# A graph layer in float32 on one core: paired row statistics, ScalarE roots, a SiLU stage of its own, and the mean taken off on VectorE

## The reference, cut to what matters

```python
def _layernorm(x, axis=-1, eps=1e-05):
    m = jnp.mean(x, axis=axis, keepdims=True)
    v = jnp.var(x, axis=axis, keepdims=True)
    return (x - m) / jnp.sqrt(v + eps)

h = jnp.maximum(_layernorm(x), 0.0)          # relu of the normalised rows
x = x + layer0(h, node_vec1, edge_attr_4, edge_attr_8, ...)
h = jnp.maximum(_layernorm(x), 0.0)
x = x + layer1(h, edge_attr_4, ...)          # h + relu(sum of messages)

# in layer0, per edge, the small net that weights the messages:
hid = jax.nn.silu(edge_scalars @ fc_w1 * (1.0 / np.sqrt(8.0)))     # 8 -> 64
weight = hid @ fc_w2 * (1.0 / np.sqrt(64.0))                       # 64 -> 192
# and per node
angle = 0.1 * (mid_s @ lin3_w) * (1.0 / np.sqrt(96.0)) * node_attr
out = jnp.cos(angle) * scfeat + jnp.sin(angle) * conv
```

## Time and profile before

| | |
|---|---|
| median of 3 runs | 2483.28 us (2479.98 to 2484.08) |
| span of the profiled execution | 2863.6 us |
| busy, of the span | PE 1940.9, PEld 1820.7, DVE 1954.7, ACT 1560.1, POOL 1745.2 us |
| instructions | PE 12874, DVE 8628, ACT 4412, POOL 1676 |
| moved | 364.52 MB |

### The profile page before, as it was taken

How to read it: one execution, slowest core, us unless ns; L and a number is a source line. 1 busy time by engine, 2 the same in 40 slices (tenths; PEclk the granted TensorE clock), 3 DMA queues, 4 the chain that set the end, 5 groups by cost and what they waited for, 6 DMA issues and landing times.

```text
span 2863.6 us, 55863 instructions
## 1 busy us (share of the span) xinstructions
PE 1940.9 (68%) x12874; PEld 1820.7 (64%) x12874; DVE 1954.7 (68%) x8628; ACT 1560.1 (54%) x4412; POOL 1745.2 (61%) x1676
## 2 busy tenths in 40 slices
PE   0888888878878888878883343434344777777877
PEld 0777777777877777777773333323233777767777
DVE  2889888887888888888884655556555444444444
ACT  0667677776777777777774444545453222222222
POOL 1656666665666666766656565655565666666665
PEclk9989999998999999999995555555555999999898
DMA  9444544443444444454543232323332333333332
GB/s 79 142 143 169 172 170 171 172 172 138 169 172 170 173 169 164 162 179 147 180 154 124 87 89 87 93 87 97 88 99 83 81 89 88 92 92 90 94 95 74
DMA packets 223602, 364.52 MB, mean 127 GB/s; under 512 B 115938, under 2 KB 133149, under 8 KB 223405
## 3 DMA queue, kind: packets, MB, share of 16 engines
q1 hardware_dynamic: 176524, 289.81, 32.1%
q0 software_dynamic: 47040, 74.31, 9.8%
HBM read 176.85 MB, written 194.78 MB: 130 GB/s over the span
## 4 chain that ended last, share of the span: by engine, by line
DVE 31%; PE 25%; issue 14%; another core or an unknown queue 11%; POOL 8%; ACT 6%; SPq 2%; DMA 1%; DVEq 1%; ACTq 0%; POOLq 0%
DVE st L1334 3%; PE bank L969 3%; PE bank L1154 3%; POOL x_e L581 3%; POOL inv L628 3%; DVE x L1353 2%; DVE su_e L1203 2%; PE bank L964 2%; PE bank L1166 2%; DVE st L1362 2%; PE bank L1163 2%; ACT h L755 2%; PE bank L1176 2%; DVE x L1599 2%
## 5 line engine op out<-in xcount | busy, mean ns | idle before, releaser
L628 POOL TENSOR_TENSOR inv<-var,minus_half 128x8 f32<-128x8 f32 x196 | 327.7, 1672 | 256.5 <-DVE var L1210 253.4
L625 POOL TENSOR_TENSOR yo<-x,h 128x640 f32<-128x640 f32 x196 | 305.8, 1560 | 147.8 <-ACT h L755 145.4
L969 PE MATMUL bank<-wp,hT 128*128 128x160 f32 x1568 | 392.6, 334 | 1.6 <-DVE x L1353 0.7
L755 ACT ACTIVATE h<-x,nmr,inv 128x160 f32<-128x160 f32 x784 | 342.2, 514 | 6.1 <-POOL nmr L642 6.1
L587 POOL DMA_INDIRECT h_all<-h,i_put x196 | 203.4, 1038 | 217.9 <-ACT h L871 146.0
L964 PE MATMUL bank<-ident,h_e 128*128 128x128 f32 x392 | 83.0, 350 | 358.9 <-ACT h_e L878 229.2
L587 POOL DMA_INDIRECT out<-yo,i_put x196 | 202.1, 1031 | 197.2 <-DVE feat L1706 63.8
L1353 DVE SCALAR_TENSOR_TENSOR x<-bank,scl,x_all 128x160 f32<-128x160 f32 x784 | 254.3, 372 | 89.1 <-PE bank L970 46.0
L969 PE MATMUL bank<-wp,eT 128*128 128x160 f32 x784 | 274.5, 444 | 54.5 <-ACT eR L886 27.3
L934 ACT ACTIVATE tot<-bank 128x160 f32<-128x160 f32 x196 | 59.6, 304 | 455.7 <-remote 207.1
L964 PEld LDWEIGHTS bank<-ident,h_e 128*128 128x128 f32 x392 | 57.5, 184 | 367.9 <-DVE hr_e L1215 244.1
(11 more groups left out here) (173 smaller groups left out, 6292.4 us busy)
## 6 DMA issues: line engine op xcount, KB each, us to landing
x_all<-in_xa SPq DMA_DIRECT2D x98, 644.0 KB, 5.8
h_all<-h SPq DMA_DIRECT2D x98, 640.0 KB, 2.9
out<-yo SPq DMA_DIRECT2D x98, 640.0 KB, 3.3
q_row<-row_tab SPq DMA_DIRECT2D x98, 256.0 KB
sum_tab<-tot SPq DMA_DIRECT2D x49, 322.0 KB, 4.2
y_tab<-yo SPq DMA_DIRECT2D x49, 320.0 KB
x<-y_tab SPq DMA_DIRECT2D x49, 320.0 KB
cv<-sum_tab SPq DMA_DIRECT2D x25, 322.0 KB
```

The lines of the kernel that those rows point to most:

```text
L625: nc.gpsimd.tensor_tensor(yo[j][:, a:b], x1[j][:, a:b], h1[j][:, a:b], ALU.add).then_inc(d_y, 1)
L628: nc.gpsimd.tensor_tensor(inv[:, 0:n], var[:, 0:n], minus_half[:, 0:n], ALU.pow).then_inc(signal, 1)
L755: ins = nc.scalar.activation(h1[j][:, k * D:(k + 1) * D], x1[j][:, k * D:(k + 1) * D], ACT.Relu, bias=nmr2[j][:, k:k + 1], scale=inv2[j][: ...
L969: nc.tensor.matmul(dst_ps, main[:, t * P:(t + 1) * P], wp[:, w:w + D], start=True, stop=False)
```

## The change

The statistics take two rows at once: the access pattern interleaves them (element 0 of row g, element 0 of row g+1, element 1 of row g, ...), so that the even half of `bn_stats` is the one row and the odd half the other. No combining is left. The root is `Sqrt` on ACT with scale 1/160 and bias eps, the inverse a `reciprocal` on DVE (in stage 1 for the dense rows; the edge rows keep the power on POOL). For dense rows and in stage 2, DVE subtracts the mean from all 160 columns; for the edge rows of stage 1 POOL does. The relu moves into the copy behind the transpose. The net's inner product and SiLU for all 49 quads stand in a stage of their own ahead of stage 1, in 13 groups, and go to a table in HBM (`hid_tab`) from which each quad loads its 128 x 256 part, behind its table loads.

```diff
-            def moment_part(part, st, su, df, sq, m2, neg, var, n, signal):
...
-            def rest_of(into, rows, neg, n, signal):
...
+            def paired_stats(st, pair, rows, width):
+                two_rows = rows[:, 2 * pair * width:(2 * pair + 2) * width].rearrange("p (g f) -> p f g", f=width)
+                return V.bn_stats(st[:, 2 * pair:2 * pair + 2, :].rearrange("p g k -> p (g k)"), two_rows[:, 0:D, :])
+            def shift_of(nmr, st, inv, n, signal):
+                V.scalar_tensor_tensor(nmr[:, 0:n], stat(st, n, 1), -1.0, inv[:, 0:n], ALU.mult, ALU.mult).then_inc(signal, 1)
...
             def dense_stats(u):
-                for k in range(GD):
-                    ins = V.bn_stats(st1[j][:, k, :], x_in[j][:, k * XW:k * XW + D])
+                for pair in range(GD // 2):
+                    ins = paired_stats(st1[j], pair, x_in[j], XW)
...
+            def dense_centre(u):
+                j, x = u.mod(2), x3(x_in[u.mod(4)], XW, GD)
+                v.wait_ge(d_ln1, u.times(1, 1))
+                wait(v, d_tr, u.times(2, -2))
+                V.tensor_tensor(x3(hb[j], P, GD), x[:, :, 32:D], bc_last(stat(st1[u.mod(4)], GD, 1), P), ALU.subtract)
+                V.tensor_tensor(x3(hr[j], 32, GD), x[:, :, 0:32], bc_last(stat(st1[u.mod(4)], GD, 1), 32),
+                                ALU.subtract).then_inc(d_cen, 1)
+            def dense_inverse(u):
+                v.wait_ge(d_sq1, u.times(1, 1))
+                V.reciprocal(inv1[j][:, :], sd1[j][:, :]).then_inc(d_scl, 1)
+            def dense_scale(u):
+                v.wait_ge(d_scl, u.times(2, 1))
+                V.tensor_tensor(scl1[j][:, :], inv1[j][:, :], x3(x_in[j], XW, GD)[:, :, D], ALU.mult).then_inc(d_scl, 1)
...
@@ POOL: p1_centre(q + 1) and p1_scale(q + 1) at the end of odd steps; dense_y(w - 3) for dense_y(w - 4)
-            def dense_scale(u):
-            def dense_norm2(u):
+            def p1_centre(q):
+                pool.wait_ge(e_ln, q.times(1, 1))
+                wait(pool, e_tr, q.times(1))
+                centre(h_e, hr_e, x_e[q.mod(2)], st_e[q.mod(2)], GQ, e_cen)
...
@@ ACT
+            def root(into, st, n, signal):
+                nc.scalar.activation(into[:, 0:n], stat(st, n, 2), ACT.Sqrt, bias=eps[:, :], scale=1.0 / D).then_inc(signal, 1)
-                nc.scalar.activation(hT[h][:, :], bank[0][:, :], ACT.Copy)
+                nc.scalar.activation(hT[h][:, :], bank[0][:, :], ACT.Relu)
...
@@ SP, between the table stores and the wait for them
+            def net_load(g):
+                n = min(GQ, Q - g * GQ)
+                wait(sp, n_mm, 2 * (g - 1))
+                sp.dma_start(n_sct[g % 2]..., scalars_t[g * GQ:g * GQ + n]...).then_inc(n_in[g % 2], 16)
+            def net_store(g):
+                sp.wait_ge(n_act, 2 * g + 2)
+                sp.dma_start(hid_tab[g * GQ:g * GQ + n]..., n_hid[g % 2]...).then_inc(n_st[g % 2], 16)
+            for g in range(NB):
+                if g + 1 < NB:
+                    net_load(g + 1)
+                net_store(g)
+            for j in range(2):
+                sp.wait_ge(n_st[j], 16 * ((NB + 1 - j) // 2))
...
+            def p1_hidden(q):
+                wait(sp, e_pw, q.times(GQ, -GQ))
+                sp.dma_start(q_hid[j][:, :], hid_tab[q.times(1)]).then_inc(e_hid[j], 16)
...
@@ PE and ACT, ahead of stage 1 (both products of 512 columns, both SiLUs of 512 columns for each group)
-            net_mm(At(0, 0, 2))
+            for g in range(-(-Q // GQ)):
+                net_mm(g)
+            pe.wait_ge(n_act, 2 * -(-Q // GQ))
...
@@ DVE step(u) of stage 1
+                if (u - 2).within(U):
+                    dense_inverse2(u - 2)          # behind x1(u-1, 0)
+                    dense_shift2(u - 2)            # behind x1(u-1, 1)
+                if u.within(U):
+                    dense_inverse(u)               # behind x1(u-1, 2)
+                    dense_scale(u)                 # behind x1(u-1, 3)
+                if ahead:
+                    dense_centre(u + 1)
-                    dense_moments(u + 1, 1) ... (2), (3), dense_rest(u + 1), dense_moments2(u - 1, 1) ... (2), (3)
...
@@ DVE p2_step(q)
-                    p2_moments(q, 1) ... (2), (3), rest_of(...), p2_moments2(q - 1, 1), (2), (3)
+                    p2_centre(q)                   # two tensor_tensor: 512 and 128 elements
```

More of the change, by code:

```diff
@@ L873, in p2_h1 @@
                 ins.then_inc(r_h1, 1)
-            def p2_relu(q):
-                act.wait_ge(r_ln1, q.times(5, 3))
-                for t in range(GQ):
-                    ins = nc.scalar.activation(h_e[:, t * P:(t + 1) * P], x_q[q.mod(4)][:, t * XW + 32:t * XW + D],
-                                               ACT.Relu, bias=neg_e[q.mod(2)][:, t:t + 1])
-                ins.then_inc(r_relu, 1)
             def p2_copy(q):
@@ L1379, in p1_stats @@
                 v.wait_ge(e_g[j], q.over(2, 64, 64))
-                for t in range(GQ):
-                    ins = V.bn_stats(st_e[j][:, t, :], x_e[j][:, t * XW:t * XW + D])
+                for pair in range(GQ // 2):
+                    ins = paired_stats(st_e[j], pair, x_e[j], XW)
                 ins.then_inc(e_ln, 1)
-            def p1_moments(q, part):
-                j = q.mod(2)
-                v.wait_ge(e_ln, q.times(5, part))
-                moment_part(part, st_e[j], su_e[j], df_e[j], sq_e[j], m2_e[j], neg_e[j], var_e[j], GQ, e_ln)
-            def p1_rest_rows(q):
-                rest_of(hr_e[q.mod(2)], x_e[q.mod(2)], neg_e[q.mod(2)], GQ, e_ln)
             def p1_selectors(q):
@@ L1525, in p2_stats, with p2_centre @@
             def p2_stats(q):
+                j = q.mod(2)
                 v.wait_ge(r_g[q.mod(4)], q.over(4, 64, 64))
-                for t in range(GQ):
-                    ins = V.bn_stats(st_e[q.mod(2)][:, t, :], x_q[q.mod(4)][:, t * XW:t * XW + D])
+                for pair in range(GQ // 2):
+                    ins = paired_stats(st_e[j], pair, x_q[q.mod(4)], XW)
                 ins.then_inc(r_ln1, 1)
-            def p2_moments(q, part):
+            def p2_centre(q):
                 j = q.mod(2)
-                v.wait_ge(r_ln1, q.times(5, part))
-                moment_part(part, st_e[j], su_e[j], df_e[j], sq_e[j], m2_e[j], neg_e[j], var_e[j], GQ, r_ln1)
+                v.wait_ge(r_ln1, q.times(1, 1))
+                wait(v, r_tr, q.times(1))
+                x = x3(x_q[q.mod(4)], XW, GQ)
+                V.tensor_tensor(x3(h_e, P, GQ), x[:, :, 32:D], bc_last(stat(st_e[j], GQ, 1), P), ALU.subtract)
+                V.tensor_tensor(x3(hr_e, 32, GQ), x[:, :, 0:32], bc_last(stat(st_e[j], GQ, 1), 32),
+                                ALU.subtract).then_inc(r_cen, 1)
             def p2_angle(q, part):
@@ L1606, in p2_stats2 @@
                 v.wait_ge(r_x1, q.times(2, 2))
-                for t in range(GQ):
-                    ins = V.bn_stats(st2[j][:, t, :], x1[j][:, t * D:(t + 1) * D])
+                for pair in range(GQ // 2):
+                    ins = paired_stats(st2[j], pair, x1[j], D)
                 ins.then_inc(r_ln2, 1)
-            def p2_moments2(q, part):
-                j = q.mod(2)
-                v.wait_ge(r_ln2, q.times(4, part))
-                moment_part(part, st2[j], su2[j], df2[j], sq2[j], m22[j], neg2[j], var2[j], GQ, r_ln2)
             def p2_norm2(q, part):
@@ L1674, in p2_step @@
                     p2_angle(q, 7)
-                if b:
-                    for part in (1, 2, 3):
-                        p2_moments2(q - 1, part)
             v.wait_ge(d_y, 2 * U)
```

290 lines of the change are left out of this document (119 added, 171 removed).

## The result

| | |
|---|---|
| before, median of 4 runs beside it | 2481.63 us (2478.22 to 2484.08) |
| after, median of 4 runs | 2458.20 us (2455.74 to 2464.43) |
| ratio | 0.9918, 95% interval 0.9896 to 0.9939 |

The kernel is 23 us (0.8%) faster; forecast were 116.

The account below looks back on a forecast made before the run. DVE was taken as nearest to full in stage 1, and stage 2 as DVE work stretched by POOL's bursts. Terms -110 - 64 + 40 = -134 us profiled, x 0.867 = -116, gave 2367 us; own range 2300 to 2430, wider range 2290 to 2570.

Parts of the forecast that it names:

- Stage 2, -64 us profiled (-55 scaled): Stage 2: less DVE work and less idle time, together -1.3 us per quad over 49 quads; bounds 0 and -179 us.
- the lock against POOL: Stage 2: DVE's small arithmetic stands idle while POOL builds descriptors, 2.1 us per quad from three rows alone.
- its floor, 10.3 us: Stage 2: POOL needs 0.99 + 0.30 us per transfer, so eight transfers per quad need 10.3 us.
- a share far from 0.867: Sign of being wrong: stage 1's share of unprofiled time far from 0.867, the unprofiled-to-profiled ratio that scaled all sums.
- The start, +40 (+35 scaled): Before stage 1: the separate SiLU stage, 13 groups at 3.1 us with nothing beside it, adds 40 us profiled.
- Stage 1, -110 (-95 scaled): Stage 1: DVE work -1.3 us and its wait on yo -0.95 us per quad, over 49 quads.
- Standing behind POOL: Stage 1: DVE instructions held while POOL reads SBUF, 2.4 us per quad, to fall by 0.4; bounds -2.4 and +1.
- The idle time, forecast -0.95: Stage 1: the 0.95 us per quad for which DVE's x1 waits on POOL's yo should go.
- What is late next is PE.: Stage 1 after the change: PE, 23.5 us of a 26.75 us quad, 88%, is the next engine to be late.
- Slow reading: Rival, stages 1 and 2: interleaved bn_stats cost extra per element; 2650 us at 0.95 ns extra; chance 0.27.
- POOL's order or PE takes the gain: Rival, stage 1: late edge-row centring on POOL, or PE stuck at 81%, leaves stage 1 unchanged; 2462 us; chance 0.15.
- Larger gain: Rival, stages 1 and 2: locks between DVE and POOL are met less often; 2240 us; chance 0.06.

Follow-up runs that it names:

- the first profile: Profile of the unedited kernel before, on which the prediction rests: an unusually slow execution, span 2863.6 us against an unprofiled median of 2483.28 us.
- the second profile: The kernel before profiled again with no edit: span 2472.0 us, time 2473.76 us.
- the kernel with y first: Kernel before with the paired statistics, and in POOL's list y(u-4) moved ahead of the power and scale of u-1: 2537.91 us (1.0229).
- the kernel with net and relus in stage 1: Changed kernel with the SiLU stage undone and the large subtractions of stages 1 and 2 back on ACT as relus: 2477.33 us (0.9991).

## Why the prediction was wrong, step by step

- **Stage 2, -64 us profiled (-55 scaled): the step that failed.** Measured +14.3 between two executions of normal length, so 70 of the 102 us between the forecast (-116) and the spans (-13.9). The prediction took 13.95 us per quad and the idle time in front of DVE's small arithmetic from the first profile, and read them as the lock against POOL. In the second profile neither is there: the quad takes 10.06 us, and POOL's eight transfers are the bound, so that less work on DVE buys nothing. The prediction had that as its floor, 10.3 us, and named it among its signs of being wrong, beside a share far from 0.867. It knew too that 380 us of the profiled span were missing from the unprofiled time, so that a stage well above its floor might be at it in the runs that count; it spread the 380 us evenly instead. The idle time of the first profile came from 18 quads of 44 (above), held up by what stays open. The loss of 14.3 us comes from the new subtraction: four scatters 0.11 us longer each are 0.44 us per quad, of which the stage shows 0.30. Undone, 17.6 us came back.
- **The start, +40 (+35 scaled).** Measured +52.1, of the right kind and too small. The 3.1 us per group came from some 6 us for a load, the products and the SiLU of a pair; the products of a pair alone take 7.2 us in line, and 3.8 per group was measured by leaving twelve groups out. The measured length lies between the sum's and that of the upper end, 4.8 us per group.
- **Stage 1, -110 (-95 scaled).** Measured -83.6, near the forecast by terms that err in both directions, which is in part luck. DVE's busy time was to fall by 1.3 us per quad and fell by 0.3, from 24.4 to 24.1. The subtraction is +2.46 for 2.4. The statistics gave about 1.1 us for 1.4, by 0.424 and 0.444 us a pair. Standing behind POOL stayed at 2.5 instead of falling by 0.4. The new small instructions cost about the 0.12 us taken, unless held (0.07 to 0.28 from start to start, 600 to 630 us). That leaves some -2.6 for the combining (an estimate), forecast -2.7. The idle time, forecast -0.95, fell by 1.4 (from 2.7 to 1.3 us per quad).
- **"What is late next is PE."** Right that PE is near: its order takes 24.3 us even with less on DVE. In the changed kernel DVE is still first, at 95%.
- **No edit in stage 3, so nothing there**: it took 7.8 us more. Over the profiles of the study, all with the same stage 3, it lies between 517.2 and 528.6 us. What moves it is open.
- **The rivals.** *Slow reading*: refuted, 0.424 us per pair. By the Trainium skill, "Vector Engine (DVE) Microarchitecture Reference", section 5.2, the second half of the rule, full rate for a stream that alternates between two regions, is the one that the trace agrees with, at 0.424 us for 320 elements that alternate between rows 161 words apart. *POOL's order or PE takes the gain*: its 2462 us are 4 from the measured 2458, but by luck. It has stage 1 as it was and 64 us won in stage 2, and the runs show the reverse, -83.6 and +14.3. POOL is idle in front of yo in the changed kernel; that POOL's order can cost much shows in the kernel with y first, 157 us. *Larger gain*: no.

What the forecast missed beyond its terms is that the parts don't add. Each row of this table differs from the one above by the parts named:

| kernel | time, us | step |
|---|---|---|
| before | 2481 | |
| + pairs | 2381 | -100 |
| + stage 1's subtraction on DVE, relu in the copy | 2486 | +105 |
| + roots on ACT, edge rows centred on POOL, stage 2's subtraction on DVE, the new order of POOL | 2393 | -93 |
| + SiLU stage = after | 2458 | +65 |

In the third row DVE takes the subtraction while POOL still has the powers; the fourth takes back most of what the third lost; the fifth avoids table loads that hurt only if ACT still has the relus, which it has not. That the order of POOL's and DVE's lists, and not one duration, makes the +105 and the -93 is argued from the waits and not shown: the parts of the fourth row weren't taken apart, and the granted clock, 1.00, 0.96 and 1.00 in the second to fourth rows, may have a share in both steps.

## What to carry to other kernels

Compare a profile's span with the unprofiled times before anything is read from it. Here they were 15% apart, and the stages were stretched by three different factors; a stage that seemed well above its floor of issue time was at it in the runs that count. Look at how often a wait occurs and how long its longest is, not only at its sum. A change of several parts is to be timed part by part, the one that only removes work first: here that part was worth 100 us, and the others gave back 77 of them, 65 by the SiLU stage and 12 by all that moves work between engines. A subtraction with two SBUF inputs, moved to DVE, also cost POOL, which it stopped.

## What the runs showed of the hardware that I had not expected

- A DVE subtraction with two inputs in SBUF holds up POOL's issue of an indirect transfer: 1.68 us for 1.00 beside a subtraction of 0.69, and 1013 to 1124 ns in the mean of scatters, back to 1013 with the subtraction on ACT. In stage 1 a gather is held too:

```profile
619.29 1.22 DVE L1336 TENSOR_TENSOR hb<-x_all,st 128x1024 f32<-128x1024 f32 x1
...
619.45 1.88 POOL L606 DMA_INDIRECT x_e<-in_xa,i_src  x1 [0.30 <-ACT h L774]
```

  The Trainium skill, "SBUF — State Buffer" (Who interferes with whom), infers that such a `tensor_tensor` doesn't slow the building of descriptors, since that needs the write side alone. For the scatters and gathers of this kernel the trace says otherwise, and the measurement decides.
- A table load on ACT takes 1283 ns, and the instructions on both sides stand close to it. ACT in the kernel with net and relus in stage 1, around one load:

```profile
803.48 0.30 ACT L812 ACTIVATE tot<-bank 128x161 f32<-128x161 f32 x1
803.80 1.28 ACT L785 ACT_TABLE_LOAD   x1
805.10 0.39 ACT L785 ACTIVATE q_hid<-bank 128x256 f32<-128x256 f32 x1
```

  The Trainium skill, "ScalarE: Activation LUTs" (What ACT_TABLE_LOAD costs), adds a drain of some 1380 ns to each switch, 2.66 us in all. The trace agrees with the 1283 ns, but here the time from the end of tot to the start of the SiLU is 805.10 - 803.78 = 1.32 us, and in all 59 loads of 400 to 1200 us the idle time in front of them sums to 1.0 us. The quad with two of them is 2.28 us longer in all.
